# A selective-state scan, worked on pairs of channel halves instead of one half at a time

## What is computed

```python
dt = softplus(dt_r @ dt_proj_w.T + dt_proj_b)          # (4, 512, 256)
dA = exp(dt[..., None] * A)                            # (4, 512, 256, 16)
dBx = dt[..., None] * Bv[:, :, None, :] * xc[..., None]
def step(h, inps):
    dA_t, dBx_t, C_t = inps
    h = dA_t * h + dBx_t
    y = jnp.einsum('bdn,bn->bd', h, C_t)
    return (h, y)
...
y = ys + xc * D
return y * silu(z) @ out_proj_w.T
```

## Time and profile before

| | before |
|---|---|
| median of 3 runs | 1762.87 us (1758.99 to 1764.25) |
| the profiled execution: its time, its span | 1760.58 us, 1758.8 us |
| busy over the span: PE, VectorE, ACT, POOL | 91%, 72%, 58%, 56% |
| mean granted clock of TensorE | 0.974 |
| scan stage, first scan to last product | 224.3 to 470.6 us, about 14% of the span |

### The profile page before, as it was taken

How to read it: one execution, slowest core, us unless ns; L and a number is a source line. 1 busy time by engine, 2 the same in 40 slices (tenths; PEclk the granted TensorE clock), 3 DMA queues, 4 the chain that set the end, 5 groups by cost and what they waited for, 6 DMA issues and landing times.

```text
span 1758.8 us, 24391 instructions
## 1 busy us (share of the span) xinstructions
PE 1605.8 (91%) x6936; PEld 1196.0 (68%) x6936; DVE 1272.3 (72%) x2156; ACT 1016.4 (58%) x2065; POOL 992.7 (56%) x955
## 2 busy tenths in 40 slices
PE   7997667877799989999899899998998999999998
PEld 5775323333367767777688677886886778878887
DVE  5555699999855756788578567885775678856665
ACT  4343655454434446676477666664776666656665
POOL 1101067766510028888433378894333888978887
PEclk9999789999999999999999999999999999999999
DMA  2000000000000036666300056663000566656674
GB/s 104 10 1 1 0 1 1 0 0 0 8 0 1 1 88 165 163 166 165 85 1 1 6 143 154 170 174 86 1 1 5 146 152 174 172 141 172 172 173 107
DMA packets 57678, 136.75 MB, mean 78 GB/s; under 512 B 10251, under 2 KB 33251, under 8 KB 57187
## 3 DMA queue, kind: packets, MB, share of 16 engines
q1 hardware_dynamic: 57571, 135.47, 30.0%
HBM read 133.33 MB, written 2.10 MB: 77 GB/s over the span
## 4 chain that ended last, share of the span: by engine, by line
PE 64%; DVE 4%; ACT 3%; issue 2%; POOL 2%; POOLq 0%; PEldq 0%; PEld 0%; DMA 0%; SPq 0%; DVEq 0%; ACTq 0%
PE ps L226 18%; PE ps L227 18%; PE ps L228 17%; PE ps L1488 2%; PE ps L1473 1%; PE ps L1474 1%; PE ps L1475 1%; PE ps L774 1%; POOL m_hc L984 1%; POOL e_lo L234 1%; PE ps L366 1%; PE ps L1476 0%; DVE p L1661 0%; PE ps L377 0%; PE ps L254 0%
## 5 line engine op out<-in xcount | busy, mean ns | idle before, releaser
L234 POOL TENSOR_TENSOR e_lo<-e_h,e_hi 128x512 fp32r<-128x512 f32 (+1 forms) x368 | 476.4, 1295 | 131.1 <-ACT e_hi L231 120.7
L1140 ACT ACTIVATE e_s<-ps 128x512 f32<-128x512 f32 (+1 forms) x368 | 220.4, 599 | 271.5 <-PE ps L228 270.8
L1296 DVE TENSOR_TENSOR ps<-e_s,ps 128x512 f32<-128x512 f32 x352 | 244.7, 695 | 179.3 <-PE ps L228 145.1
L226 PE MATMUL ps<-xn_hi,eh 128*128 128x512 f32 x704 | 284.8, 405 | 10.3 <-ACT e_s L1140 7.4
L227 PE MATMUL ps<-xn_lo,eh 128*128 128x512 f32 x704 | 279.5, 397 | 0.0
L228 PE MATMUL ps<-xn_hi,el 128*128 128x512 f32 x704 | 278.8, 396 | 0.0
L1301 DVE TENSOR_TENSOR e_h<-ps,rwb 128x512 f32<-128x512 f32 x352 | 243.3, 691 | 16.2 <-DVE ps L1296 4.8
L984 POOL TENSOR_TENSOR m_hc<-m_h,m_c 128x512 f32<-128x512 f32 x128 | 172.5, 1348 | 125.3 <-DVE m_h L940 122.9
L234 POOL TENSOR_TENSOR el<-e_raw,eh 128x128 fp32r<-128x128 f32 (+1 forms) x352 | 221.8, 630 | 26.7 <-ACT eh L1129 26.7
L231 ACT ACTIVATE e_hi<-e_h 128x512 fp32r<-128x512 f32 (+1 forms) x368 | 229.3, 623 | 7.4 <-DVE e_h L1301 7.3
L774 PE MATMUL ps<-m_hc,const 128*128 128x512 f32 x256 | 149.5, 667 | 48.8 <-POOL m_hc L984 43.9
(11 more groups left out here) (232 smaller groups left out, 3293.5 us busy)
## 6 DMA issues: line engine op xcount, KB each, us to landing
e_raw<-in_experts SPq DMA_DIRECT2D x176, 192.0 KB, 3.9
rwb<-rw_rows SPq DMA_DIRECT2D x64, 352.0 KB
rwb<-rw_rows SPq DMA_DIRECT2D x80, 256.0 KB
rwb<-rw_rows SPq DMA_DIRECT2D x32, 320.0 KB
rwb<-rw_rows SPq DMA_DIRECT2D x48, 192.0 KB
rwb<-rw_rows SPq DMA_DIRECT2D x32, 224.0 KB
rwb<-rw_rows SPq DMA_DIRECT2D x32, 160.0 KB
rwb<-rw_rows SPq DMA_DIRECT2D x80, 64.0 KB
```

The lines of the kernel that those rows point to most:

```text
L226: pe.matmul(out, w_hi, x_hi, start=start, stop=False, skip_group_check=True)
L234: return eng.tensor_tensor(lo, full, hi.bitcast(F32), ALU.subtract)
L1140: act.activation(e_s[0:rows_, buf, :], ps[0:rows_, 4, :], ACT.Silu).then_inc(S["silu"], 1)
L1296: dve.tensor_tensor(ps[:, bank, :], e_s[:, buf, :], ps[:, 5, :], ALU.mult).then_inc(S["gated"], 1)
```

## The change: what it does

One item is now one state with both halves (`n`, 64 items). `input_term` writes both halves of a state to two neighbouring PSUM banks (0 and 1, or 6 and 7, in turn) from one bank of B; one scan runs over the 1024 elements, with the decay of the second half's first token set to 0 by a memset, so that the recurrence starts anew there (ACT writes only the 511 others); POOL's product has 1024 elements, reading C twice. PE spreads B once for each state. The B bank is one, C stays in bank 2, and the output projection now goes into bank 2 too. Buffers are two states deep as before. `HEAD` is 5 states, and the closing steps stand after states 1, 2 (gate, and `g_hi` on ACT), 3 (`g_lo`, projection) and 4 (residual sum).

```diff
-        ITEMS, HEAD = DS * MC, 8
-        DEEP = 4
-        B_BANKS, C_BANK, SPREAD_AHEAD = (0, 1, 3, 7), 2, 3
+        HEAD = 5
+        DB_BANKS, B_BANK, C_BANK = (0, 6), 3, 2
+
+        def both(tile, n):
+            return tile[:, MC * (n % 2):MC * (n % 2) + MC, :]
...
+        def terms(n):
+            first_bank = DB_BANKS[n % 2]
+            return ps[:, first_bank:first_bank + MC, :]
+
+        def of_both(v):
+            return v.unsqueeze(1).broadcast_to([P, MC, T])
...
         def mix_pe(pe, L):
...
+            def spread_b(i, blk, n):
+                after(pe, "db", DS * i + n)
+                pe.matmul(ps[:, B_BANK, :], sel_bc[:, n, :], bc[:, blk], start=True, stop=True).then_inc(M["b_spread"], 1)
...
+            def item(i, blk, n, last):
                 following = bass.ds((i + 1) * T, T)
+                if n + 2 < DS:
+                    spread_b(i, blk, n + 2)
                 elif not last:
+                    spread_b(i + 1, following, n + 2 - DS)
+                if n == HEAD - 1:
+                    after(pe, "x_new", i)
+                    spread_c(i, blk, n)
+                if n + 1 < DS and n + 1 != HEAD - 1:
                     spread_c(i, blk, n + 1)
...
+                if n:
+                    total(i, n - 1)
...
+            def total(i, n):
+                pe.wait_ge(*M("hc", DS * i + n + 1))
+                for m in range(MC):
+                    if n == 0:
+                        after(pe, "ylin", 2 * i + m - 1)
+                    last = pe.matmul(ps[:, 4 + m, :], ident, both(m_hc, n)[:, m, :], start=(n == 0), stop=(n == DS - 1),
+                                     skip_group_check=True)
+                last.then_inc(M["y_sum"], 1)
...
         def mix_act(act):
...
+                after(act, "h", DS * i + n - 1)
+                for m in range(MC):
+                    act.activation(both(m_da, n)[:, m, m:T], dt_b[:, m, m:T], ACT.Exp,
+                                   scale=neg_a[:, m * DS + n:m * DS + n + 1]).then_inc(M["da"], 1)
+                act.wait_ge(*M("c_spread", DS * i + n + 1))
+                after(act, "hc", DS * i + n - 1)
+                act.activation(m_c[:, n % 2, :], ps[:, C_BANK, :], ACT.Identity).then_inc(M["c_copy"], 1)
+
+            def finish(i, blk, n):
+                if n == 2:
                     after(act, "out", i)
...
         def mix_dve(dve):
...
+            def input_term(i, blk, n):
+                dve.wait_ge(*M("b_spread", DS * i + n + 1))
+                after(dve, "h", DS * i + n - 1)
+                dve.tensor_tensor(terms(n), du[:, :, blk], of_both(ps[:, B_BANK, :]), ALU.mult).then_inc(M["db"], 1)
...
+                dve.wait_ge(*M("da", 2 * (DS * i + n + 1)))
+                dve.wait_ge(*M("db", DS * i + n + 1))
+                after(dve, "hc", DS * i + n - 1)
+                dve.tensor_tensor_scan(in_line(both(m_h, n)), in_line(both(m_da, n)), in_line(terms(n)), 0.0,
                                        ALU.mult, ALU.add).then_inc(M["h"], 1)
 
+                if isinstance(i, int) and i == 0 and n + 1 < NB:
+                    softplus_end(n + 1)
+                    dt_times_xc(n + 1)
...
         def mix_pool(pool):
...
+            def item(i, blk, n, last):
+                pool.wait_ge(*M("h", DS * i + n + 1))
+                pool.wait_ge(*M("c_copy", DS * i + n + 1))
+                after(pool, "y_sum", DS * i + n - 1)
+                pool.tensor_tensor(both(m_hc, n), both(m_h, n), of_both(m_c[:, n % 2, :]), ALU.mult).then_inc(M["hc"], 1)
```

More of the change, by code:

```diff
@@ L205, in program @@
             "bc_hi bc_lo v nabs e ln dt du b_spread c_spread da db h c_copy hc y_sum ylin "
-            "gated g_hi g_lo out x_new aexp bc_zero dt_b").split(), 0), 1)
+            "gated g_hi g_lo out x_new aexp bc_zero dt_b da_zero").split(), 0), 1)
         A, = group("att", dict.fromkeys((
@@ L768, in item @@
                     spread_c(i, blk, n + 1)
-                elif m == 0 and not last:
+                elif n + 1 == DS and not last:
                     spread_c(i + 1, following, 0)
[L771 to L775, removed]
@@ L777, in finish @@
-            def finish(i, blk, q):
-                if q == 4:
-                    after(pe, "x_new", i)
+                if n:
+                    total(i, n - 1)
+                elif not (isinstance(i, int) and i == 0):
+                    total(i - 1, DS - 1)
+            def total(i, n):
[6 more added lines that the diff above has]
+                last.then_inc(M["y_sum"], 1)
@@ L780, in finish @@
+            def finish(i, blk, n):
+                if n == 0 and isinstance(i, int):
+                    total(i, DS - 1)
+                if n == 3:
+                    pe.wait_ge(*M("c_copy", DS * NB if isinstance(i, int) else DS * (i + 1) + HEAD - 1))
                     for m in range(MC):
@@ L782, in finish @@
                         w = slice(M_OUT + m * P, M_OUT + (m + 1) * P)
-                        last = mm3(pe, ps[:, 6, :], mh[:, w], ml[:, w], g_hi[:, m, :], g_lo[:, m, :], m == 0, m == MC - 1)
+                        last = mm3(pe, ps[:, C_BANK, :], mh[:, w], ml[:, w], g_hi[:, m, :], g_lo[:, m, :], m == 0, m == MC - 1)
                     last.then_inc(M["out"], 1)
@@ L929, in item @@
+            def item(i, blk, n, last):
                 following = bass.ds((i + 1) * T, T)
-                if q == ITEMS - 2 and not last:
-                    dve.wait_ge(*M("da", 32 * i + ITEMS))
+                if n == DS - 1 and not last:
+                    dve.wait_ge(*M("da", 2 * DS * (i + 1)))
                     dt_copy(i + 1, following)
-                if q + 1 < ITEMS:
-                    input_term(i, blk, q + 1)
+                if n + 1 < DS:
+                    input_term(i, blk, n + 1)
@@ L941, in item @@
+                dve.tensor_tensor_scan(in_line(both(m_h, n)), in_line(both(m_da, n)), in_line(terms(n)), 0.0,
                                        ALU.mult, ALU.add).then_inc(M["h"], 1)
-                if isinstance(i, int) and i == 0 and q < HEAD:
-                    if q % 2 == 0 and q // 2 + 1 < NB:
-                        softplus_end(q // 2 + 1)
-                    if q % 2 == 1 and q // 2 + 1 < NB:
-                        dt_times_xc(q // 2 + 1)
-                    if q == HEAD - 1:
+                if isinstance(i, int) and i == 0 and n + 1 < NB:
+                    softplus_end(n + 1)
+                    dt_times_xc(n + 1)
+                    if n + 2 == NB:
```

90 lines of the change are left out of this document (30 added, 60 removed).

## The result

The changed kernel takes 1794.17 us, the median of 4 runs (1792.37 to 1796.05), against 1762.51 of the kernel before on the same chip (4 runs). The ratio is 1.0182, 95% interval 1.0163 to 1.0201: slower by some 32 us, where +20 was forecast. The time is in the predicted range, 1764 to 1798, near its upper end.

A forecast was written before the change was run, and what follows sets the result against it. The prediction took VectorE's gapless stream to bound the scan stage. Its terms summed to +20.0 us on the profiled 1760.6, giving 1780.6; with the median 2.3 higher, it said 1781.5, range 1764 to 1798.

The forecast's parts named there:

- longer instructions: VectorE's input terms and scans of 1024 elements save 0.10 us for each of 64 states: -6.4 us.
- wait on the scan just before: VectorE's input term waits for the scan right in front, 0.11 us more in 44 places: +4.8 us.
- gate: ACT's `g_hi` stands before the decay of state 3, so VectorE waits 0.9 us in each of 3 blocks: +2.7.
- bank 2: C of state 4 waits for the residual sum, delaying ACT's decay of state 5: +3.7 us over 3 blocks.
- POOL and the pairs: POOL's longer product goes between VectorE's two gate or `g_lo` products, four of six pairs, 1.07 us more each: +4.3.
- softplus pairs: Two neighbouring VectorE softplus steps, three times, let POOL's product in between, 2.14 us each: +6.4 us.
- projection waits: VectorE's wait of 0.53 us behind the projection's matmuls, coming twice, is hidden behind longer states: -1.1 us.
- tail: After the last scan, POOL's product, PE passes and first half's sum delay the second half's sum: +2.5 us.
- PE low clock: PE at 1.2 GHz around the residual sum makes B for state 7 late, in two of three blocks: +2.8 us.
- VectorE keeps its port: Rival: POOL never gets between VectorE's paired products, so those losses go; 1767 us, chance 0.20 (wholly or mostly).
- large fixed part of the scan: Rival: VectorE's scan has a large fixed cost, so 64 joined scans save 35 us more; 1746 us, chance 0.10.
- long stretch at the low clock: Rival: PE stays at the low clock for half of the scan stage, +35 us; 1816 us, chance 0.10.

The follow-up runs named there:

- three pairs deep: Changed kernel without PE's sums over the states, input terms kept in three pairs of PSUM banks instead of two; 1778.42 us, ratio 1.0094 to the kernel before.
- POOL in halves: Changed kernel with POOL's product as two instructions of 512 elements, each with its own signal; 1783.67 us, ratio 1.0125 to the kernel before.
- pairs in one: Changed kernel with the gate and `g_lo` each one VectorE instruction of 1024 elements instead of two of 512; 1779.95 us, ratio 1.0101 to the kernel before.

## Why the prediction was near, and low

The direction, the place and each mechanism came as told. The gap of 11 us in the stage is nearly all in three terms that were sized too low. (The sum itself comes to 1782.9, 1780.6 and the 2.3 by which the median lies higher; the 1781.5 that was said has no reason given.) From rows, start to start, for the stage (3.308 is the period of the run three pairs deep, where nothing waits; what a state takes above it is the wait):

| term | forecast | measured | from |
|---|---|---|---|
| longer instructions | -6.4 | -6.9 | 64 x (3.308 - 3.416) |
| wait on the scan just before | +4.8 | +9.4 | 44 x (3.521 - 3.308) |
| gate | +2.7 | +2.6 | 3 x 0.87 |
| bank 2 | +3.7 | +5.4 | 1.87, 1.86, 1.69 |
| POOL and the pairs | +4.3 | +8.6 | 6 x 2.15 - 4 x 1.07 |
| softplus pairs | +6.4 | +6.5 | 3 x 2.18 |
| start | +0.3 | +0.4 | 0.89 - 0.46 |
| projection waits | -1.1 | -1.1 | none left |
| tail | +2.5 | +3.4 | 11.1 - 7.7 |
| PE low clock | +2.8 | +2.5 | 0.60, 0.82, 1.10 |
| sum | +20.0 | +30.8 | stage: +30.8 |

- **The wait on the scan just before** is the step that failed most. I took the 0.03 after the record's end from the dt copy behind the softplus step, the only row with a dependent neighbour. Behind a scan it is 0.10, and the waiting instruction itself takes 0.02 more. (Three of the 44, the input terms of state 1 behind a dt copy and a scan, start only 0.03 after the record's end, as 293.92 + 2.28 to 296.23; why stays open.) It turns the whole idea: the long instructions save 6.9 us and the two-deep banks cost 9.4, so even the bare loop is slower. The run three pairs deep shows this.
- **POOL and the pairs**: I carried the share of lost pairs over, four of six. In the changed kernel POOL went between in all six, and in the three softplus pairs, and with its product cut back to 512 elements it still did, nine times of nine. So it wasn't the longer product that lost the two pairs more. Its hold was priced right, as the run with POOL in halves shows by its size and the run with pairs in one by its end. Why VectorE won two pairs in block 0 of the kernel before stays open: POOL's product started 0.31 after the gate in both blocks of the earlier trace rows.
- **Bank 2**: the sum took the spreading of C at 0.40, full clock; PE was at 0.50 there and took 0.80. I had priced the low clock in the next term and not in this one. That is 0.40 of the 0.6 by which blocks 0 and 1 came out dearer; another 0.2 is the start of the scan, which follows the end of the second exponential (323.97 + 1.32) by 0.22. In the third block, where the term is 1.69, it follows by 0.03, as I had taken it. Why stays open.
- **PE's low clock**: the sum agrees by luck. I took two blocks of 1.4; it was all three, of 0.60 to 1.10.
- The rivals. VectorE keeps its port: no pair shows it. A large fixed part of the scan: it is 0.05, and the break-even was 0.36. The long stretch at the low clock didn't come: from 222 to 502 us the clock is 0.87, in block 0 it is back at 1.00 from 328 on, and the pace of 3.52 held. (At the start it was low for some 20 us longer than before, beside VectorE's stream, at the cost of some 0.2 us before 256.99 and 258.31.) The rule on instructions that exclude each other for their whole length, from the Trainium skill (SBUF — State Buffer, section Who interferes with whom), agrees with 3.34, 2.26 and 1.11. What the Trainium skill says of the scan's half throughput (DVE: opcode table, instruction layouts, handler registers and perf-mode slots, section 6, Datapath and trigger behaviour) agrees with 1.07 for 512 elements against the product's 0.53.

## What to carry to other kernels

Making instructions longer saves only their fixed part, here 0.05 us each on VectorE, and asks for buffers that are as many instructions deep as before, not as many bytes: two deep in states meant one instruction deep in waits, and a wait on the instruction right in front cost 0.21 a state where the longer instructions save 0.11. Where VectorE has neighbouring products with both inputs in SBUF while POOL has work waiting, each gap between them can cost a whole POOL instruction, so it pays to join VectorE's pair (13.1 us of the stage here), and it costs to lengthen POOL's. When a wait is taken away and another engine was late by nearly as much, the gain is only the difference; look for who is next before pricing the repair.

## What the runs showed of the hardware that was not expected

- An input term that waits for the scan right in front of it starts 0.10 us after the scan's record ends, one that doesn't 0.09 before: 0.19, and it takes 1.14 itself and not 1.12. Behind the softplus step the same kind of wait had 0.03.
- POOL took every gap that was offered in the changed kernel, nine of nine, with products of 1024 elements and of 512 alike; before the change it had four of six. The hold goes both ways: with the pairs in one, POOL's product beside the gate is on record with 3.27 us and not 2.36.
- With the sums gone, PE worked at 0.50 through the stage, and VectorE waited for B only once, 0.9 us at the start, with 3.52 us for a state.
